# Edge pass of a two-layer graph network: bias in the table's rows, earlier head sums, wide weighed additions

## The reference, cut to what matters

```python
h = (x_flat @ W_gat).reshape(M, HEADS, NUM_EXPERTS)          # 4 heads x 4 experts
e = leaky_relu(a_src[src] + a_dst[dst], negative_slope=0.2)  # 524288 edges and the loops
ee = exp(e - e_max[dst])
alpha = ee / (denom[dst] + 1e-16)
agg = segment_sum(h[src] * alpha[:, :, None], dst).reshape(M, 16) + b_gat
scores = layernorm(agg, ln_gamma, ln_beta).reshape(M, HEADS, NUM_EXPERTS).mean(1)
topk_s, topk_i = top_k(scores, 2);  w = softmax(topk_s)
for ei in range(4):
    g = where(topk_i == ei, w, 0.0).sum(-1)
    hh = gelu(x @ W1[ei] + b1[ei], approximate=False)
    out = out + g[..., None] * (hh @ W2[ei] + b2[ei])
```

## Time and profile before

| | |
|---|---|
| median of three runs | 3117.63 us |
| span of the profiled execution | 3601.8 us, 31245 instructions |
| difference of the two | 484.2 us |
| DVE busy | 2257.8 us (63%), 4422 instructions |
| PE busy | 1935.1 us (54%) |
| POOL busy | 1857.5 us (52%) |
| ACT busy | 1215.1 us (34%) |

### The profile page before, as it was taken

How to read it: one execution, slowest core, us unless ns; L and a number is a source line. 1 busy time by engine, 2 the same in 40 slices (tenths; PEclk the granted TensorE clock), 3 DMA queues, 4 the chain that set the end, 5 groups by cost and what they waited for, 6 DMA issues and landing times. The chain is left out here.

```text
span 3601.8 us, 31245 instructions
## 1 busy us (share of the span) xinstructions
PE 1935.1 (54%) x8829; PEld 1316.8 (37%) x8829; DVE 2257.8 (63%) x4422; ACT 1215.1 (34%) x2447; POOL 1857.5 (52%) x1723
## 2 busy tenths in 40 slices
PE   1776642387878645567432455454544444454555
PEld 1555542255655434456311222232222222222223
DVE  8999886989999965554223454454553444544547
ACT  2676754244444323455311122122212122121222
POOL 5400248554544444445575656655655656656561
PEclk9998865699999867777555676676776677767768
DMA  5792001011111121101111111111111111111111
GB/s 198 250 391 84 16 23 39 24 40 37 46 44 41 36 60 40 56 20 23 42 27 23 32 33 32 32 28 38 32 33 32 32 28 31 38 28 32 37 29 30
DMA packets 170130, 192.35 MB, mean 53 GB/s; under 512 B 59241, under 2 KB 126096, under 8 KB 169008
## 3 DMA queue, kind: packets, MB, share of 16 engines
q1 hardware_dynamic: 107616, 118.69, 9.9%
q0 software_dynamic: 57088, 62.48, 8.4%
q10 hardware_dynamic: 5328, 9.97, 0.7%
HBM read 91.70 MB, written 105.25 MB: 55 GB/s over the span
## 5 line engine op out<-in xcount | busy, mean ns | idle before, releaser
L1518 POOL DMA_INDIRECT edge_rows<-node_table,edge_ids x1024 | 1006.5, 983 | 646.2 <-POOLq L1243 345.9
L1646 PE MATMUL x_b_hid<-x_featT,x_w 128*128 128x512 f32 x512 | 362.3, 854 | 281.4 <-PEq L1243 93.5
L1146 POOL DMA_INDIRECT token_results<-arena,token_of x160 | 251.1, 1569 | 294.3 <-ACT arena L1082 216.9
L583 DVE TENSOR_TENSOR sort_ping<-sort_pong 128x1024 f32<-128x1024 f32 (+1 forms) x232 | 395.1, 1744 | 11.3 <-issue 3.8
L1158 POOL DMA_INDIRECT arena<-keys,row_ids x256 | 249.3, 974 | 288.6 <-DVE counts L821 181.0
L583 DVE TENSOR_TENSOR sort_pong<-sort_ping 128x1024 f32<-128x1024 f32 (+1 forms) x230 | 389.9, 1736 | 8.7 <-ACT sort_ping L1016 3.7
L1139 POOL DMA_INDIRECT slots<-arena,send x128 | 177.8, 1389 | 371.9 <-ACT arena L1038 336.9
L1640 PE MATMUL x_b_featT<-ident,x_feat 128*128 128x128 f32 x128 | 34.8, 428 | 581.0 <-issue 385.3
L1653 PEld LDWEIGHTS x_b_res<-x_w,x_hid 128*128 128x128 f32 x2048 | 276.1, 216 | 152.1 <-issue 152.1
L1653 PE MATMUL x_b_res<-x_w,x_hid 128*128 128x128 f32 x2048 | 303.9, 307 | 39.8 <-issue 39.8
L1646 PEld LDWEIGHTS x_b_hid<-x_featT,x_w 128*128 128x128 f32 x512 | 118.9, 262 | 500.2 <-issue 300.9
(11 more groups left out here) (346 smaller groups left out, 4059.0 us busy)
## 6 DMA issues: line engine op xcount, KB each, us to landing
edge_table<-zeros SPq DMA_DIRECT2D x8, 5120.0 KB, 35.7
edge_rows<-node_table,edge_ids POOLq DMA_INDIRECT x1024
arena<-slots SPq DMA_DIRECT2D x40, 260.0 KB
slots<-zeros SPq DMA_DIRECT2D x2, 5120.0 KB, 24.4
edge_table<-edge_rows SPq DMA_DIRECT2D x64, 160.0 KB
out_dram<-x_y ACTq DMA_DIRECT2D x33, 256.0 KB
x<-in_x_dram SPq DMA_DIRECT2D x4, 2048.0 KB, 20.2
adjacent<-in_adj_dram SPq DMA_DIRECT2D x32, 256.0 KB, 2.7
```

Of the source, the lines that this page charges most:

```text
L583: step(dve.tensor_tensor(vb[:, :, t, :], va[:, :, 0, :], va[:, :, 1, :], op))
L1146: pool.indirect_dma_start(rows_dram, bass.IndirectOffsetOnAxis(token_of[:, n % 4, r:r + 1], 0), res[:, n % 2, r, :], None, bounds_check=TO ...
L1518: pool.indirect_dma_start(rows[:, u, c, :], None, table_dram, bass.IndirectOffsetOnAxis(ids[:, u, c:c + 1], 0)).then_inc(rows_in[u], 16)
L1646: pe.matmul(b_hid[:, c % 2, :], w1[:, c // HC1, c % HC1 * P:(c % HC1 + 1) * P], featT[:, :], start=True, stop=True).then_inc(hid_mm, 1)
```

## The change

The bias `gat_b` is no longer added at L1435. It is loaded in `front` into `row_bias` (with eight zeros behind it) and added to the 24 numbers of each table row while they are copied out of PSUM (L389). After the squares, the product with gamma is taken before the root is known; its head sums are made beside the variance sum, and the root and the sum of beta are then applied to 4 numbers a node where there were 16. The sixteen weighed additions become one product of 128x2048 out of PSUM, two additions between SBUF tiles (128x1024 and 128x512) and one addition of `x` (128x512). `res_free` is given right behind the product. The tile `weighed` grows from 512 to 2048 numbers a partition.

```diff
@@ Projection.dve
-        dve.tensor_scalar(self.into[:, n * PER:(n + 1) * PER, :], self.b_out[n % 2][:, :, 0:self.cols], 1.0, None, ALU.mult).then_inc(self.kept, 1)
+        dve.tensor_tensor(self.into[:, n * PER:(n + 1) * PER, :], self.b_out[n % 2][:, :, 0:self.cols],
+                          self.bias.unsqueeze(1).to_broadcast([P, PER, self.cols]), ALU.add).then_inc(self.kept, 1)
@@ front, vector
+            link(dve.memset(row_bias[:, GAT:TAB], 0.0))
-            dve.wait_ge(gat_in, 32)
+            dve.wait_ge(gat_in, 48)
@@ front, sync
             sp.dma_start(gat_w[:, 0:GAT], a["gat_w"]).then_inc(gat_in, 16)
+            sp.dma_start(row_bias[:, 0:GAT], across(a["gat_b"], GAT)).then_inc(gat_in, 16)
@@ edges_and_experts1, vector, ahead of the loop
-            dve.wait_ge(consts_in, 64)
+            dve.wait_ge(consts_in, 48)
+            link(dve.tensor_reduce(beta_sum[:, :], beta[:, :].rearrange("p (h e) -> p e h", h=HEADS), AX_X, ALU.add))
@@ turn
-                then(dve.tensor_tensor(A, A, each16(gat_b[:, :]), ALU.add))
 
                 then(dve.tensor_reduce(mean[:, :], A, AX_X, ALU.add))
                 then(dve.scalar_tensor_tensor(A, per16(mean[:, :]), 1.0 / GAT, A, ALU.mult, ALU.subtract))
-                then(dve.tensor_tensor(B, A, A, ALU.mult))
-                then(dve.tensor_reduce(var[:, :], B, AX_X, ALU.add))
+                step(dve.tensor_tensor(B, A, A, ALU.mult))
+                step(dve.tensor_tensor(G, A, each16(gamma[:, :]), ALU.mult))
+                settle()
+                step(dve.tensor_reduce(var[:, :], B, AX_X, ALU.add))
+                step(dve.tensor_reduce(s4[:, :, :], G.rearrange("p n (h e) -> p n e h", h=HEADS), AX_X, ALU.add))
+                settle()
...
-                then(dve.tensor_tensor(A, A, per16(root[:, :]), ALU.mult))
-                then(dve.tensor_tensor(A, A, each16(gamma[:, :]), ALU.mult))
-                then(dve.tensor_tensor(A, A, each16(beta[:, :]), ALU.add))
-                then(dve.tensor_reduce(s4[:, :, :], A.rearrange("p n (h e) -> p n e h", h=HEADS), AX_X, ALU.add))
+                then(dve.tensor_tensor(s4[:, :, :], s4[:, :, :], per4(root[:, :]), ALU.mult))
+                then(dve.tensor_tensor(s4[:, :, :], s4[:, :, :], beta_sum[:, :].unsqueeze(1).to_broadcast([P, UNIT, E]), ALU.add))
...
-                for e in range(E):
-                    if e == E - 1:
-                        take(dve, out_done, 16)
-                    for v in range(UNIT):
-                        so_far = x[:, bass.ds(unit * UNIT + v, 1), :].rearrange("p o f -> p (o f)") if e == 0 else weighed[:, v, :]
-                        to = y[:, v, :] if e == E - 1 else weighed[:, v, :]
-                        last = dve.scalar_tensor_tensor(to, b_res[:, e, v, :], one[:, v, e:e + 1], so_far, ALU.mult, ALU.add)
-                        step(last)
-                    settle()
+                then(dve.tensor_tensor(weighed[:, :, :, :], b_res[:, :, :, :],
+                                       one[:, :, :].rearrange("p v e -> p e v").unsqueeze(3).to_broadcast([P, E, UNIT, FEAT]), ALU.mult))
+                dve.sem_inc(res_free, 1)
+                then(dve.tensor_tensor(weighed[:, 0:2, :, :], weighed[:, 0:2, :, :], weighed[:, 2:4, :, :], ALU.add))
+                then(dve.tensor_tensor(weighed[:, 0, :, :], weighed[:, 0, :, :], weighed[:, 1, :, :], ALU.add))
+                take(dve, out_done, 16)
+                then(dve.tensor_tensor(y[:, :, :], x[:, mine, :], weighed[:, 0, :, :], ALU.add))
                 dve.sem_inc(summed, 1)
-                dve.sem_inc(res_free, 1)
@@ edges_and_experts1, sync
-            for to, of in ((gat_b, "gat_b"), (gamma, "gamma"), (beta, "beta")):
+            for to, of in ((gamma, "gamma"), (beta, "beta")):
```

More of the change, by code:

```diff
@@ L353, with __init__ @@
 class Projection:
-    def __init__(self, sem, tag, x, rstd, shift, ident, weight, cols, into, view, banks, lo=0, turned_in=(0, 1), put_in=(2, 3)):
+    def __init__(self, sem, tag, x, rstd, shift, ident, weight, cols, into, bias, view, banks, lo=0, turned_in=(0, 1), put_in=(2, 3)):
         self.feat, self.featT = view(lo, 2, PER, FEAT), view(lo + 1024, 2, PER, NODES)
@@ L359, in __init__ @@
             sem(f"{tag}_{n}") for n in ("normed", "turned", "featT", "projected", "kept"))
-        self.x, self.rstd, self.shift, self.ident, self.weight, self.cols, self.into = x, rstd, shift, ident, weight, cols, into
+        self.x, self.rstd, self.shift, self.ident, self.weight, self.cols, self.into, self.bias = x, rstd, shift, ident, weight, cols, into, bias
     def act_step(self, act, n, u):
@@ L411, in front @@
         gate_w, gate_b = sb("gate_w", [P, EXPERTS]), sb("gate_b", [P, EXPERTS])
+        row_bias = sb("row_bias", [P, TAB])
         gat_w, att, att_part = sb("gat_w", [P, TAB]), sb("att", [P, 2, GAT]), sb("att_part", [P, 2, GAT])
@@ L471, in front @@
         LAG, CHUNK = 12, GROUPS // 4
-        gat = Projection(sem, "gat", x, rstd, shift, ident, gat_w[:, :], TAB, tab, view, banks, 4112, (1, 1), (3, 3))
+        gat = Projection(sem, "gat", x, rstd, shift, ident, gat_w[:, :], TAB, tab, row_bias[:, :], view, banks, 4112, (1, 1), (3, 3))
         gat_norms = []
@@ L1197, in edges_and_experts1 @@
         msg, got, sums, adv = sb("win_msg", [P, UNIT, WINDOW, GAT]), sb("win_got", [P, UNIT, GAT]), sb("win_sums", [P, UNIT, HEADS]), sb("win_adv", [P, PAIRS])
-        gat_b, gamma, beta = sb("gat_b", [P, GAT]), sb("gat_gamma", [P, GAT]), sb("gat_beta", [P, GAT])
-        whole, agg, square = sb("gat_whole", [P, UNIT, HEADS]), sb("gat_agg", [P, UNIT, GAT]), sb("gat_square", [P, UNIT, GAT])
+        gamma, beta, beta_sum = sb("gat_gamma", [P, GAT]), sb("gat_beta", [P, GAT]), sb("gat_beta_sum", [P, E])
+        whole = sb("gat_whole", [P, UNIT, HEADS])
+        agg, square, scaled = (sb(f"gat_{n}", [P, UNIT, GAT]) for n in ("agg", "square", "scaled"))
         mean, var, root, half, first = (sb(f"gat_{n}", [P, UNIT]) for n in ("mean", "var", "root", "half", "first"))
@@ L1208, in edges_and_experts1 @@
         feat, featT = sb("x1_feat", [P, UNIT, FEAT]), sb("x1_featT", [P, SPAN])
-        hid, weighed, y = sb("x1_hid", [P, E * HC1, SPAN]), sb("x1_weighed", [P, UNIT, FEAT]), sb("x1_y", [P, UNIT, FEAT])
+        hid, weighed, y = sb("x1_hid", [P, E * HC1, SPAN]), sb("x1_weighed", [P, E, UNIT, FEAT]), sb("x1_y", [P, UNIT, FEAT])
         b_next, b_featT, b_hid, b_res = ps("b_next", [P, 512]), ps("x1_b_featT", [P, UNIT, P]), ps("x1_b_hid", [P, 2, SPAN]), ps("x1_b_res", [P, E, UNIT, FEAT])
@@ L1359, in _ @@
             by_head = sc[:, :, :, :].rearrange("p t k h -> p t h k")
-            A, B = agg[:, :, :], square[:, :, :]
+            A, B, G = agg[:, :, :], square[:, :, :], scaled[:, :, :]
             def per16(ap):
```

## The result

The changed kernel takes 3155.86 us (median of 4 runs, 3154.1 to 3159.22) against 3117.32 for the kernel before, a ratio of 1.0128 with a 95% interval of 1.0114 to 1.0143: 38.5 us slower, where 22 were forecast.

The account below looks back on a forecast made before the run. POOL's calls were taken to bound the 30 turns: 3117.6 + 30 x 0.75 for held calls - 0.5 for DVE's shorter last two turns = 3140 us, 0.7% slower. The forecast's own range was 3124 to 3165, the wider one 3105 to 3167.

Parts of the forecast that it names:

- POOL holds the turn: 30 turns of the edge pass: POOL's 34 calls set the timed turn of 38.8 us; DVE has 7.5 us slack.
- The 484 us lie in the 30 turns; a timed call takes 1.08 us: Edge pass: the profile's extra 484.2 us sit in turns with POOL calls; a timed call takes 1.08 us, not 1.25.
- the takes: POOL's turn in the edge pass: about 1 us a turn beside the 34 calls, counted into the profiled 44.6 us.
- the faster rival: Edge pass: DVE holds the turn in timed runs too, giving 3017 us, or 3110 with no stretch to lose; chance 0.22.
- Calls are held by two SBUF inputs and released 0.81 us behind: POOL calls started during a DVE instruction with two SBUF inputs last until 0.81 us after it; PSUM input costs nothing.
- Price 0.75 us a turn: Three wide SBUF additions: POOL's held calls cost 0.75 us a turn, taken between 0.5 and 0.9; bounds 0 to 1.6.
- The worked meeting: Wide additions: the first costs a call 0.51 us in the mean, the last 0.37, together 0.9 us a turn.
- a mean price over all such instructions: Second way to the price: 0.19 us for each us of SBUF-twice instructions, so 2.6 us more cost 0.5 a turn.
- Nearly sure to be hit, whatever the rhythm: First wide addition (128x1024): catches a call's start with a chance of 1.08/1.14, against the no-change rival (0.14).
- Gates 0.6 us shorter, additions 0.35 longer, DVE 0.25 shorter: DVE's turn: gates save 0.6 us, wide additions lose 0.35, net 0.25 shorter; worth -0.5 us in all under POOL's bound.
- Front nothing: Front, with L389's second operand, a small memset and a small DMA: 0 us taken, at most 0.7.
- A profiled span near 3345: Whole profile after: fewer stretched semaphore increments on DVE shorten the span by 261 us to near 3345, while the time rises.

Follow-up runs that it names:

- e5_dummy_psum: The kernel before plus one idle 128x1024 addition a turn behind the sixteen, one input in PSUM and one in SBUF: 1.0002 of before.
- e1_sixteen: The changed kernel with its four wide additions put back to the sixteen of before: 3114.8 us, 1.0002 of before.
- e2_wide_only: The kernel before with only the sixteen additions made four wide ones: 3131.3 us, 1.0056 of before.
- e11_later_both: The changed kernel with three tiny idle DVE instructions ahead of the product and two ahead of the addition of `x`: 3118.9 us, 1.0008 of before.
- e4_dummy_sbuf: The kernel before plus one idle 128x1024 addition a turn behind the sixteen, both inputs in SBUF: 1.0010 of before.

## Why the prediction was right, point by point

- *POOL holds the turn.* Right: POOL waits 20.2 us in the whole span, DVE 500.9 for windows, and up to 1.26 us more of DVE work in each turn costs nothing (e5_dummy_psum).
- *The 484 us lie in the 30 turns; a timed call takes 1.08 us.* Wrong. The first turn begins at 1749.2 us after, against 1887.1: some 138 us of the stretch lay in front. The turn of before must be 43.3 us, not 38.8 (e1_sixteen, equal in time, has 43.25), a call and the gap behind it take 1.25 us also in profiles as long as the timed runs, and the takes cost 0, not 1 us. The bound survived this because the turn without POOL's bound, 34.1 rather than 31.3, is still 9 us shorter; the point from which the faster rival decides, 1.07 us a call, was never near.
- *Calls are held by two SBUF inputs and released 0.81 us behind.* Right, to 0.02 us: in the additions of all kernels it is 0.81 to 0.83. What the Trainium skill ("SBUF — State Buffer", "Who interferes with whom") says of two SBUF inputs agrees with 1.61 against 0.94; its inference that descriptor generation isn't held up by `tensor_tensor` doesn't.
- *Price 0.75 us a turn.* This is the term that was mis-sized: it measured 1.13 at the additions and 0.3 elsewhere. The worked meeting gave 0.9, and for the last addition 0.37 where 0.44 was measured; I pulled it down by a mean price over all such instructions (0.5), taken besides from the stretched profile: its calls were held for 1.2 us a turn, those of e1_sixteen for 0.78. A mean has no meaning where each turn repeats one meeting: 0.07 and 0.69 are both real, 0.6 us of program apart. I had written that the meeting repeats and then not used it.
- *"Nearly sure to be hit, whatever the rhythm".* Wrong, and here luck comes in. The same three additions cost 1.13 us a turn in the changed kernel, 0.51 in e2_wide_only and 0.02 in e11_later_both, by their place against the calls alone. The forecast didn't work that place out. That the change came out slower and not the same was forecast from the right mechanism, but the place that made it so was not foreseen.
- *Gates 0.6 us shorter, additions 0.35 longer, DVE 0.25 shorter.* The additions take 2488.12 to 2493.47, 5.35 us and not 5.1. The last whole turn is 31.0 against 31.3. With half the calls the change brings 0.58 us a turn, more than 0.25, because the additions aren't on the circle of DVE and ACT that holds that turn.
- *Front nothing.* Right: L389 takes 0.250 us against 0.256. Turn 1 begins at 1749.2 us in after and 1752.2 in e1_sixteen, and at 1749.4, 1752.2 and 1747.2 in e2_wide_only, e4_dummy_sbuf and e5_dummy_psum, which have the front of before.
- *A profiled span near 3345.* Wrong, since the stretch didn't come back: 3154.0.

## What to carry to other kernels

Where POOL issues indirect DMAs without a pause, the costly thing on a vector engine with slack is not its instructions' length but which of them read two SBUF operands when a call begins; a PSUM operand takes the cost away even when the work grows. Long instructions of that kind fix the rhythm of both engines against each other, so price a new one by the place where a call will meet it in the actual sequence, not by a mean. And before leaning on gaps of a profile whose span is far from the timed runs, find the stages where it is longer: here both the loop and 138 us of front were.

## What the runs showed of the hardware

- A call (128 rows of 80 bytes) takes 0.944 us and the next begins 0.30 behind it: 34 of them and the held time give the turn to 0.05 us in every kernel of the table, and their profiles are as long as the timed runs to 6 us.
- Calls held by an addition end 0.81 to 0.83 us behind it; so a start in its last 0.13 us loses nothing, and calls begun that late in a score instruction do last 0.94. A call begun ahead of such an instruction is through, even where it begins only 2 to 10 ns ahead (16 times in e1_sixteen, 0.94 to 0.95 each; the vector instruction then takes 0.02 to 0.03 us more, 1.51 to 1.52 instead of 1.49 for a message product).
- One profiled execution can be 484 us longer than the timed ones, some 138 us of it in the front and some 350 in the 30 turns; thirteen others were not. Its cause stays open.
